# Attention's rotation split over three engines: VectorE multiplies by the cosines, ScalarE copies the swapped halves out of PSUM, GpSimd multiplies by the sines and adds

## The reference

```python
q = rope(x @ Wq.T); k = rope(x @ Wk.T); v = x @ Wv.T       # x is normalised
# rope: x * cos + concat([-x[..., 64:], x[..., :64]]) * sin
scores = einsum('bhnid,bhnjd->bhnij', qc, kc)
y_intra = (scores * decay) @ xc
state_{c+1} = state_c * exp(G_last) + k_dec.T @ xc
y = y_intra + (qc * exp(G)) @ state
y = y / rms(y) * gnorm_w * silu(x @ Wg.T)
out = x + y @ Wo.T                                        # then the feed-forward layer
```

## Time and profile before

| what | value |
|---|---|
| time, median of 3 runs | 1896.69 us (1889.1 to 1899.47) |
| the profiled execution: its own time / its span | 1899.84 us / 1898.1 us |
| busy share PE, DVE, ACT, POOL | 96%, 67%, 36%, 34% |
| mean granted TensorE clock | 0.985 of full speed |
| first and last `k_turn` of the attention stage | 73.39 us, 1354.88 us |

### The profile page before, as it was taken

The page is one execution under the profiler, slowest core; times in us unless marked ns, Lnnn a source line. Parts: engine busy times, 40 slices in busy tenths (PEclk is TensorE's granted clock), DMA queues, the critical chain, the costliest instruction groups (busy, mean ns, idle before and its releaser), DMA issues.

```text
span 1898.1 us, 27791 instructions
## 1 busy us (share of the span) xinstructions
PE 1823.5 (96%) x8856; PEld 1479.9 (78%) x8856; DVE 1271.2 (67%) x2340; ACT 692.1 (36%) x2186; POOL 644.5 (34%) x741
## 2 busy tenths in 40 slices
PE   6799999999999999999999999999979999999997
PEld 5578878787887787788787878888757888888885
DVE  7777877787787778778777867887765333333332
ACT  4533443443344444334444433443443211212111
POOL 3444444443444434444444434444411011010110
PEclk9899999999999999999999999999989999999998
DMA  4132332233233223323322232322455232322321
GB/s 157 46 106 76 97 100 62 66 96 106 70 101 103 62 63 100 106 72 99 103 63 70 95 102 69 100 72 66 145 193 167 68 100 82 96 86 80 100 80 32
DMA packets 111073, 173.54 MB, mean 91 GB/s; under 512 B 8016, under 2 KB 45904, under 8 KB 110928
## 3 DMA queue, kind: packets, MB, share of 16 engines
q1 hardware_dynamic: 110928, 171.80, 31.0%
HBM read 133.50 MB, written 38.27 MB: 90 GB/s over the span
## 4 chain that ended last, share of the span: by engine, by line
PE 75%; DMA 7%; DVE 5%; issue 4%; SPq 2%; ACT 2%; POOL 2%; ACTq 0%; DVEq 0%; POOLq 0%
PE p_proj L84 25%; PE p_kept L84 10%; PE p_tok L1236 9%; PE p_kept L1236 9%; DMA g_row<-g_scratch 6%; PE p_y L705 4%; PE p_score L84 4%; PE p_cst L690 4%; PE p_y L704 3%; PE p_qa L84 3%; PE p_f L1402 2%; SPq L609 2%; POOL q L113 1%; PE p_tok L673 1%; DVE z L848 1%
## 5 line engine op out<-in xcount | busy, mean ns | idle before, releaser
L113 POOL TENSOR_TENSOR q<-rope_a,rope_b 128x512 f32<-128x512 f32 x128 | 166.5, 1301 | 348.7 <-DVE rope_b L105 213.8
L84 PE MATMUL p_proj<-shared,wq_hi 128*128 128x512 f32 x744 | 251.9, 399 | 0.0
L84 PE MATMUL p_proj<-wg_hi,shared 128*128 128x512 f32 x528 | 189.8, 440 | 0.0
L942 ACT ACTIVATE probs<-g_row,stab 128x128 f32<-128x128 f32 x512 | 163.9, 402 | 57.9 <-POOL g_row L1064 57.9
L705 PE MATMUL p_y<-v_tok,probs 128*128 128x128 f32 x1024 | 182.2, 275 | 0.0
L84 PE MATMUL p_proj<-shared,wkv_hi 128*128 128x512 f32 x496 | 172.8, 410 | 0.0
L84 PE MATMUL p_kept<-wg_hi,shared 128*128 128x512 f32 x496 | 168.1, 420 | 0.0
L967 ACT ACTIVATE square<-p_y 128x128 f32<-128x128 f32 x512 | 134.2, 279 | 87.5 <-PE p_y L705 81.6
L84 PEld LDWEIGHTS p_proj<-shared,wq_hi 128*128 128x128 f32 x744 | 139.9, 188 | 32.3
L848 DVE SCALAR_TENSOR_TENSOR z<-p_y,srstd,gate 128x128 f32<-128x128 f32 x512 | 143.5, 341 | 27.7 <-issue 20.4
L705 PEld LDWEIGHTS p_y<-v_tok,probs 128*128 128x128 f32 x1024 | 150.1, 192 | 2.9
(11 more groups left out here) (198 smaller groups left out, 4204.9 us busy)
## 6 DMA issues: line engine op xcount, KB each, us to landing
g_row<-g_scratch SPq DMA_DIRECT2D x128, 256.0 KB, 6.0
z_scratch<-z_st SPq DMA_DIRECT2D x256, 128.0 KB
w_raw<-z_scratch SPq DMA_DIRECT2D x62, 512.0 KB, 6.6
e_row<-e_scratch SPq DMA_DIRECT2D x96, 256.0 KB, 4.0
w_raw<-in_wq_t SPq DMA_DIRECT2D x16, 512.0 KB, 8.2
w_raw<-in_wg_t SPq DMA_DIRECT2D x16, 512.0 KB, 5.7
w_raw<-in_wo_t SPq DMA_DIRECT2D x12, 512.0 KB, 6.0
w_raw<-in_wkv_t SPq DMA_DIRECT2D x8, 512.0 KB, 5.1
```

The source lines that it names most:

```text
L84: mm = pe.matmul(out, lhs[a], rhs[e], start=(i == 0 and j == 0), stop=(i == len(pairs) - 1 and j == 2))
L113: pool.tensor_tensor(out, keep["rope_a"][:, s, :], keep["rope_b"][:, s, :], ALU.add).then_inc(keep["roped"], 1)
L942: e = act.activation(probs[:, c % 2, h, :], g_row[:, c % 2, h, :], ACT.Exp, bias=stab[:, b % 2, c, T_BIAS, h:h + 1])
```

## The change: what it does

In `attention_stage` (not in `norm_stage`, whose rotations keep `rotate` and `add_rope`) a rotation becomes five instructions on three engines. DVE keeps `rope_a` = x * cos. ScalarE copies the two halves of the unit out of PSUM, swapped, into `rope_b` (`swap_halves`, after a wait for DVE's product), and now signals `rope_terms`. POOL multiplies `rope_b` by the sines in place, waits for that on its own semaphore, and adds (`rotated`).

```diff
-                rotate(dve, keep, bank(n, b, at), (b + 1 + r) % 2)
+                dve.tensor_tensor(keep["rope_a"][:, (b + 1 + r) % 2, :], bank(n, b, at)[:, :, :].rearrange("p h t -> p (h t)"),
+                                  keep["cos"][:, :], ALU.mult).then_inc(rope_cos, 1)
...
+            def swap_halves(n, b, at, r):
+                if not ahead(n):
+                    return
+                act.wait_ge(rope_cos, ROPED * n + r + 1)
+                half, x = D // 2, bank(n, b, at)[:, :, :].rearrange("p h t -> p (h t)")
+                rope_b = keep["rope_b"][:, (b + 1 + r) % 2, :]
+                act.activation(rope_b[0:half, :], x[half:D, :], ACT.Copy)
+                act.activation(rope_b[half:D, :], x[0:half, :], ACT.Copy).then_inc(rope_terms, 1)
...
                 make_decay(n, b, 1)
+                swap_halves(n, b, K_UNIT, 0)
                 make_tanh(g, b, n, 0)
...
+                    swap_halves(n, b, Q_UNIT[c - 1], c)
                     make_tanh(g, b, n, c)
+                swap_halves(n, b, Q_UNIT[2], 3)
                 squares(n, 2)
+                swap_halves(n, b, Q_UNIT[3], 4)
                 if ahead(n):
                     k_high(n + 1, b + 1)
...
+            def rotated(n, b, r):
+                s = (b + r) % 2
+                rope_b = keep["rope_b"][:, s, :]
+                pool.wait_ge(rope_terms, ROPED * n + r + 1)
+                pool.tensor_tensor(rope_b, rope_b, keep["sin"][:, :], ALU.mult).then_inc(rope_sin, 1)
+                pool.wait_ge(rope_sin, ROPED * (n - 1) + r + 1)
+                out = k[:, b % 2, :] if r == 0 else q[b % 2][:, r - 1, :]
+                pool.tensor_tensor(out, keep["rope_a"][:, s, :], rope_b, ALU.add).then_inc(roped, 1)
...
-                    add_rope(pool, keep, n + 1, b + 1, 3)
+                    rotated(n + 1, b + 1, 3)
                     row_landed(n + 1, 1)
-                    add_rope(pool, keep, n + 1, b + 1, 4)
+                    rotated(n + 1, b + 1, 4)
```

More of the change, by code:

```diff
@@ L470, in attention_stage @@
         unit_done, score_done, y_done = sem("unit_done"), sem("score_done"), sem("y_done")
+        rope_cos, rope_sin = sem("rope_cos"), sem("rope_sin")
         cst_done, tok_done = sem("cst_done"), sem("tok_done")
@@ L1098, in step @@
                 if ahead(n):
-                    add_rope(pool, keep, n + 1, b + 1, 0)
+                    rotated(n + 1, b + 1, 0)
                 mask(n, 2)
@@ L1104, in step @@
                 if ahead(n):
-                    add_rope(pool, keep, n + 1, b + 1, 1)
+                    rotated(n + 1, b + 1, 1)
                 mask(n, 3)
@@ L1110, in step @@
                     step_tables(g if b < B - 1 else g + 1, (b + 1) % B, n + 1)
-                    add_rope(pool, keep, n + 1, b + 1, 2)
+                    rotated(n + 1, b + 1, 2)
                     mask(n + 1, 0)
```

## The result

| | before | changed |
|---|---|---|
| median, us (runs) | 1897.10 (4) | 1942.95 (4) |
| lowest to highest, us | 1889.10 to 1899.47 | 1937.05 to 1946.40 |
| profiled execution: own time; span, us | 1899.84; 1898.1 | 1937.05; 1935.3 |
| mean granted clock of TensorE | 0.985 | 0.978 |

The changed kernel is slower, by a ratio of 1.0246 [1.0207, 1.0285]: 46 us of median where the prediction had 30. Its profiled execution was the fastest of its four, and the profiled one of the kernel before was slow among its own, so between the two traces there are 37 us to find, not 46.

A forecast was written before the change was run, and what follows sets the result against it. PE, busy 96% of the span, was taken as the bound, so other engines count only where PE waits. Terms of 9.6, 11.4, 6.3 and 3.4 summed to 30.7 us, from 1896.69 to 1927 us; range 1898 to 1957.

The forecast's parts named there:

- The forecast case: Longer rotations make PE wait in the attention stage: 1927 us, 1.6% slower; chance 0.62.
- Hidden: Rival: ordinary steps keep within their 1.33 us cover and b = 0 effects cancel, 1894 to 1903 us; chance 0.17.
- Faster: Rival: VectorE's savings bring the third `state` earlier in b = 0 steps, shrinking stalls, 1879 us; chance 0.08.
- Much slower: Rival: GpSimd's added products hold up VectorE's two-input instructions in every rotating step, 37 us more, 1964; chance 0.13.
- 1. ordinary steps: End of 16 ordinary steps: PE waits for `v_t` behind the longer rotation chain, 0.6 us each, 9.6 us.
- 2. b = 0, six steps: Third `state` 0.5 us late, row following, plus 1.38 us on GpSimd behind the landing: 1.9 each, 11.4 us.
- 3. b = 3, seven steps: Third `state` and row landing unmoved; GpSimd's product comes behind the landing, 1.3 us more per step.
- 3. wait for `state` gone: At the chunk state in b = 3 steps, PE's 0.30 us idle and 0.1 restart vanish, 0.4 us per step.
- step 0: First b = 0 step: VectorE has slack, so 1.4 us saved and 1.38 added cancel.
- 4. clock: TensorE's granted clock falls after two more b = 0 waits of over 3 us, 1.7 us each: 3.4 us.
- The signs I named: Profile: copies about 0.6 us, `squares` waiting for `rope_a`, product near 1.3, 20 or more `v_t` waits, clock below 0.985.
- one sign of being wrong: In b = 0 steps, rows landing much earlier than 9 us after the third `state`'s issue chain allows.

The follow-up runs named there:

- experiment 2: Changed kernel without GpSimd's product (sines left out), keeping the cosine product, two ScalarE copies and one addition: 1881.52 us, 0.9906.
- experiment 5: Changed kernel with GpSimd's 128x512 product replaced by a power of 128x5 elements, sines left out: 1932.81 us, 1.02.
- 4: Changed kernel with the wait for the row of g_row moved between GpSimd's product and addition of the fourth query: 1918.39 us, 1.0104.
- 7: Changed kernel with the wait for the row of g_row moved behind the fourth query's addition, carried by a tiny addition: 1901.16 us, 1.0036.
- experiment 8: Kernel before the change with only the wait for the row of g_row moved behind the fourth query's addition, carried by a tiny addition: 1870.11 us, 0.9859.
- Experiment 3: Changed kernel with squares(n, 2) put ahead of the third query's copies on ScalarE, as before the change: 1926.71 us, 1.0147.
- Experiment 6: Changed kernel with rms of chunks 0 and 1 ahead of the rotations of the key and first query on GpSimd: 1936.05 us, 1.0217.
- experiment 10: Changed kernel with squares(n, 2) ahead of the third query's copies and the row's wait behind the last addition, rms unmoved: 1875.26 us, 0.9884.

## Why the prediction was right in direction and short in size

The forecast case came true: slower, within the range. None of the rivals did. *Hidden* fell with the ordinary steps, which all wait. *Faster* was right that relief of VectorE is worth something, and experiment 2 shows it, 16 to 18 us, but only without the product. *Much slower* took the holds for the multiplier; product and addition stayed at 1287 and 1348 ns, below its mark of 1.6 us, and experiment 5 bounds what holds cost at 10 us. The Trainium skill (GPSIMD Engine Reference, Specifications) states the shared SBUF interface behind those holds; the trace agrees on `k_lo`, 692 ns beside a 128x5 operation against 989 beside the 128x512 one. It was the wrong place to look for the large risk.

Here is the sum term by term, by `k_turn` to `v_turn` of the steps in both traces. From the first `k_turn` to the last the attention took 1281.5 us before and 1321.3 after, 39.8 us more (2.6 us of it are given back outside this stretch).

| term | predicted, us | read from the traces, us |
|---|---|---|
| 1. ordinary steps | 16 x 0.6 = 9.6 | 16 x 0.87 = 13.9 |
| 2. b = 0, six steps | 6 x 1.9 = 11.4 | 47.6 - 45.7 = 1.9 |
| 3. b = 3, seven steps | 7 x 1.3 = 9.1 | 52.6 - 36.1 = 16.6 |
| 3. wait for `state` gone | -2.8 | 7 x -0.41 = -2.9 |
| step 0 | 0 | -0.2 |
| 4. clock | 3.4 | 39.8 less the others: 10.5 |

The `v_turn` of step 30, 1.15 us later than before, lies behind the last `k_turn`. The -0.41 is the stretch from the `v_turn` of a step with b = 2 to the next `k_turn`, 36.05 us before and 35.64 after: 0.3 of idle time and 0.1 of restart, as predicted.

Part of the hit is luck. Term 2 was 9.5 us too high and the b = 3 part of term 3 was 7.5 too low, and the two nearly cancel. With only the first put right the sum would have been 21.2 us, with only the second 38.2, against the 39.8 read. The direction and the path through GpSimd's queue are not luck: experiments 2, 4, 7 and 8 show them.

**Ordinary steps.** The order was read rightly: copies in front of the squares, squares in front of the fourth query. Experiment 3 undoes just that and gets all of it back. Short were two sizes. The pair of copies takes 1.20 us (880.61 to 881.81) and not 1.1, twice on this path. The addition behind `k_lo` takes 1.60 us and not 1.30, in every ordinary step, which I had counted at a part. The chain without a hold gave 0.36; with 0.2 and 0.3 it is 0.86, and the trace has 0.87. Of the 0.87, 0.70 is idle time of PE; the other 0.17 are the restart. In the gapless run `v_turn` starts at 864.01, before the end of the matmul ahead of it (863.78 + 0.39); behind a wait nothing overlaps.

**Steps with b = 3, the step that failed.** The prediction said, "I take the third `state` as unmoved by the same two effects, so the landing (903.01) stays". It moved: that is the step that was wrong. Before, `state` of step 19 started 8.96 us ahead of `k_turn` (891.08 and 900.04), after, 7.41 (914.32 and 921.73). Averaged over the seven, the landing frees GpSimd 3.70 us behind `k_turn` instead of 2.50. That is 1.2, and product with its semaphore is 1.35 behind it; 0.2 was cover. The chain between shows how GpSimd's product gets into a row's time without touching it; the changed kernel, step 19:

```profile
897.67 1.28 POOL L1103 TENSOR_TENSOR rope_b<-rope_b,sin 128x512 f32<-128x512 f32 x1 [4.98 <-ACT rope_b L980]
899.03 1.30 POOL L1106 TENSOR_TENSOR k<-rope_a,rope_b 128x512 f32<-128x512 f32 x1
900.28 1.09 POOL L1079 TENSOR_SCALAR_AFFINE_SELECT g_row<-g_row 128x512 f32<-128x512 f32 x1
901.35 0.63 POOL L1095 TENSOR_TENSOR svar<-ssum,eps 128x4 f32<-128x4 f32 x1
902.06 1.02 POOL L1097 TENSOR_TENSOR srstd<-svar,mhalf 128x4 f32<-128x4 f32 x1
903.16 1.12 DVE L850 SCALAR_TENSOR_TENSOR z<-p_y,srstd,gate 128x128 f32<-128x128 f32 x4 [1.25 <-issue]
904.21 0.68 DVE L788 TENSOR_TENSOR rope_a<-p_kept,cos 128x512 f32<-128x512 f32 x1
```

Product, addition, mask, `svar`, `srstd` stand gapless in one queue; `z` waits for it on VectorE, the next cosine product behind `z`, the next product on GpSimd behind that, and it goes around twice before the third `state` lets SyncE store and load. I had worked this loop out for b = 0 and not applied it to b = 3. Experiment 6 confirms it: with the norms ahead of product and addition the third `state` came 1.8 us earlier.

**Steps with b = 0** were overestimated, 11.4 us against 1.9: here the landing was wrong. The product behind the row costs its 1.35 us there too, but the row frees GpSimd earlier, 4.11 us behind `k_turn` on average instead of 5.16, and 1.35 less 1.05 is the 0.3 us per step that the table shows. Term 2 had the third `state` half a microsecond late; it starts 9.8 us ahead of `k_turn` on average instead of 9.9. In step 12 it ends at 613.05 and SyncE issues the row at 618.00, about as far behind it as before (600.29 and 605.61), but the row then frees GpSimd after 7.7 us and not 9.3. These steps' PE had been held up at the end of the step before, so `k_turn` and `state` are both late in absolute time.

**Clock.** Expected were two more falls. The windows of 6 us from the `v_turn` of the changed kernel, of which two with b = 3, one with b = 0 and the deepest (PE busy ... PEclk, DMA share, GB/s):

```profile
413.00:419.00 6.00, 6.00 (x22) 4.68 (x22) 3.69 (x5) 4.95 (x16) 2.86 (x4) 0.72 0.05 15
757.00:763.00 6.00, 6.00 (x27) 4.63 (x28) 3.74 (x5) 4.74 (x16) 2.65 (x4) 1.00 0.07 15
629.00:635.00 6.00, 5.49 (x20) 4.60 (x21) 3.19 (x7) 3.77 (x15) 3.23 (x4) 0.72 0.03 10
974.00:980.00 6.00, 5.62 (x16) 4.57 (x17) 3.15 (x8) 3.65 (x15) 3.23 (x4) 0.50 0.01 3
```

Before, 4 of the 14 windows at steps that end with a row were below 1.00, all with b = 0; after, 11 of 14, five of them with b = 3, where PE had never waited over 0.4 us at `v_turn`. At 0.50 it is the level of 1.2 GHz for the whole window, at 0.72 for part of it. The length of the wait does not settle which: 2.85 us in step 15 (756.88) left the clock at 1.00, 2.26 us in step 19 took it to 0.72. PE's busy time over the stretch of the table, before and after:

```profile
73.39:1354.88 1281.49, 1261.23 (x6203) 1021.84 (x6204) 1004.96 (x1896) 526.84 (x1897) 557.17 (x650) 0.99 0.31 86
71.80:1393.12 1321.32, 1274.20 (x6204) 1031.31 (x6205) 814.31 (x1587) 704.76 (x2200) 778.52 (x804) 0.98 0.28 84
```

It grew by 13.0 us, of which 2.3 are restarts (3.1 at later `v_turn`s, less 0.8 where the wait for `state` went). So the clock cost 10.7 us by this count and 10.5 by the remainder in the table, three times what I had put. The price of one fall was right: in the five steps with b = 3 the way from `v_turn` to the next `k_turn` grew by 1.3 to 1.6 us each (by 2.4 and 2.8 behind the two deepest, with b = 0), and the prediction had 1.7. Wrong was the number of falls, because no step with b = 3 was expected to fall.

**The signs I named** held: copies of 0.60 us, squares of chunk 2 waiting, product 1.29, 31 waits for `v_t`, ordinary ones of 0.7 us, `state` gone, clock 0.978. Only steps with b = 0 waited 1.5 to 3.7 us instead of 3 to 6. And one sign of being wrong came true in part: rows in b = 0 steps landed sooner than the 9 us after their issue, 7.7 us in step 12, and term 2 fell by it.

**What is not settled**: why a row in a step with b = 0 lands sooner after its issue, by 1.6 us in step 12. What the transfers ahead of it have to do with that I did not try. Nor was the 0.2 us that ordinary steps still wait in experiment 2 taken apart.

The best version measured is experiment 8, the kernel before with only the row's wait moved: 1870.11 us. The changed kernel with both orders mended (experiment 10) is 5 us above it on the same chip (six runs each, 1871.31 to 1877.24 against 1868.45 to 1872.63). So all but 5 of the 46 us lost were a matter of order in two queues, yet nothing measured here speaks for the change.

## What to carry to other kernels

Before work is moved to another engine, read that engine's queue at the critical place and look for a wait on a DMA: all that stands behind it pays for the landing, needed or not. Put such a wait right ahead of the one instruction that needs it; here that move, at the price of one small addition per step (median 0.65 us in the kernel before, 0.20 in the changed one), was worth 27 us to the kernel before and 42 to the changed one. And an operation added to a queue is priced around the whole loop, through what it makes late on other engines until the next DMA is issued, in every kind of step and not only in the one where the stall is now.

## What the runs showed of the hardware that was not expected

- GpSimd's queue is served in order, so a wait that the instruction behind it doesn't need still holds it. Experiments 7 and 8 measure it at 42 and 27 us. The Trainium skill (PSUM — Partial Sum Buffer, Engine vs sequencer instructions) says that the queues of ScalarE, VectorE and GpSimd are strictly first in, first out; these runs agree.
- Two copies of 64x512 from PSUM on ScalarE, 0.60 and 0.59 us, follow each other after 0.61 us. A `tanh` of 128x512 ahead of `k_tok` is followed after 0.49. Half the partitions save no time here, and there was no overlap.
- A power of 128x5 elements takes GpSimd 1169 ns, nearly the 1287 of a product of 128x512.
- After a wait of PE of 3.2 us (step 20 of the changed kernel) the granted clock averaged 0.50 over the next 6 us, the lower level throughout. After 2.85 us (step 15) it stayed at 1.00.
